# Three phases of an attention kernel merged into one order of slots, with queries and keys projected separately and their scores row-tiled

## The reference, cut to what matters

```
mod = silu(c) @ wmod ; sa, ca, ga, sb, cb, gb = its six parts, one row for each batch
h = layernorm(x) * (1 + ca) + sa
x = x + ga * causal_attention(h)                       # one head of 128: "phase A"
h = layernorm(x) * (1 + cb) + sb
# the light attention, "phase L": windows of 128 rows, 8 heads
q, k, v = rmsnorm(h) @ wq, split(rmsnorm(h) @ wkv)
light = softmax(q k^T / 8) v @ wo                      # in each window and head
# the routing: 2 score vectors of 256 for each batch, 32 in all
for token in (q_token, kv_token):
    s = h @ token
    scores = coor_descent(s)                           # 50 iterations over 32 x 256 numbers
    top_k(scores)                                      # 128 rows as queries; all 256 as keys
# the heavy attention, "phase H": 128 chosen queries against 256 keys, 8 heads
heavy = softmax(q_h k_h^T / 8) (v_h * scores_kv) @ wo_h
x = x + gb * (light + heavy added to the chosen rows)
```

## Time and profile before

| | |
|---|---|
| median of 3 runs | 541.76 us (539.86 to 545.21) |
| profiled execution, its own time | 540.5 us |
| its span, first to last instruction | 538.7 us |
| granted TensorE clock, mean | 0.981 |
| PE busy | 480.9 us (89%), 3805 matmul instructions |
| DVE busy | 387.7 us (72%) |
| ACT busy | 396.4 us (74%) |
| POOL busy | 259.9 us (48%) |

### The profile page before, as it was taken

One profiled execution on the slowest core, in us unless ns is written; L12 is line 12 of the kernel. 1 busy time (PEld: TensorE's weight loads), 2 busy tenths in 40 slices (PEclk: granted clock), 3 DMA queues, 4 the chain that ended last, 5 costly groups with the idle time before them and its releaser, 6 DMA issues.

```text
span 538.7 us, 12047 instructions
## 1 busy us (share of the span) xinstructions
PE 480.9 (89%) x3805; PEld 414.2 (77%) x3805; DVE 387.7 (72%) x1311; ACT 396.4 (74%) x1480; POOL 259.9 (48%) x294
## 2 busy tenths in 40 slices
PE   2498878766999999999999798899999999999995
PEld 1386656545888888888888676798898988888984
DVE  5539999985888888888888798365656656556652
ACT  2269899856999999999999567666666676666662
POOL 6316577772334333334433123454556665556555
PEclk9999999978999999999999889999999999999998
DMA  8740101100000000000000000000000100000101
GB/s 233 258 204 2 31 21 31 31 30 19 2 12 12 12 11 11 12 11 12 11 12 12 12 10 12 21 19 8 12 12 11 16 16 12 12 12 11 16 7 16
DMA packets 18398, 16.42 MB, mean 30 GB/s; under 512 B 1984, under 2 KB 17104, under 8 KB 18080
## 3 DMA queue, kind: packets, MB, share of 16 engines
q1 hardware_dynamic: 14336, 11.83, 6.8%
q0 software_dynamic: 3248, 3.41, 3.7%
q10 hardware_dynamic: 752, 0.40, 0.3%
HBM read 10.36 MB, written 5.28 MB: 29 GB/s over the span
## 4 chain that ended last, share of the span: by engine, by line
PE 69%; DVE 7%; ACT 2%; issue 1%; POOL 1%; POOLq 0%; DVEq 0%
PE bank L651 13%; PE bank L653 10%; PE bank L652 10%; PE bank L884 6%; PE bank L932 6%; PE bank L834 6%; PE bank L916 5%; PE bank L852 5%; PE bank L819 4%; PE bank L949 2%; ACT pr L584 1%; DVE left L1250 1%; DVE top_at L1251 1%; DVE nmx L1218 1%; DVE top_all L1247 1%
## 5 line engine op out<-in xcount | busy, mean ns | idle before, releaser
L402 POOL TENSOR_TENSOR pr<-pr,rinv 128x512 f32<-128x512 f32 x64 | 66.7, 1042 | 134.8 <-DVE rinv L1224 134.7
L417 POOL TENSOR_TENSOR pr<-pr,rinv 128x512 f32<-128x512 f32 x64 | 72.5, 1133 | 76.6 <-DVE rinv L1327 76.4
L584 ACT ACTIVATE pr<-bank,nmx 128x128 f32<-128x128 f32 x256 | 89.7, 364 | 8.0 <-DVE nmx L1218 7.9
L628 ACT ACTIVATE pr<-bank,nmx 128x256 f32<-128x256 f32 x128 | 59.7, 472 | 34.0 <-DVE nmx L1321 33.9
L1218 DVE TENSOR_REDUCE nmx<-bank 128x4 f32<-128x512 f32 x64 | 43.5, 680 | 28.8 <-PE bank L653 27.2
L584 ACT ACTIVATION_READ_ACCUMULATOR pr<-bank,nmx 128x1 f32 x256 | 52.5, 205 | 0.0
L819 PE MATMUL bank<-ident,pr 128*128 128x128 f32 x256 | 39.6, 278 | 5.8 <-POOL pr L402 5.8
L1321 DVE TENSOR_REDUCE nmx<-bank 128x2 f32<-128x512 f32 x64 | 43.8, 684 | 0.7 <-PE bank L653 0.4
L884 PE MATMUL bank<-xq,T_w 128*128 128x128 f32 x256 | 41.8, 286 | 0.4 <-ACT xq L613 0.4
L638 ACT ACTIVATE pt<-bank 128x512 f32<-128x512 f32 x64 | 38.4, 600 | 1.4 <-PE bank L916 1.4
L916 PE MATMUL bank<-ident,pr 128*128 128x128 f32 x256 | 38.5, 273 | 0.4 <-POOL pr L417 0.4
(11 more groups left out here) (231 smaller groups left out, 1506.9 us busy)
## 6 DMA issues: line engine op xcount, KB each, us to landing
mod_bc<-mod_rows_scratch SPq DMA_DIRECT2D x1, 3072.0 KB, 11.1
X<-in_L_attn_x SPq DMA_DIRECT2D x4, 512.0 KB, 10.3
xh_scratch<-xhs SPq DMA_DIRECT2D x16, 128.0 KB, 1.8
out<-X SPq DMA_DIRECT2D x16, 128.0 KB, 1.8
mod_bc<-mod_rows_scratch SPq DMA_DIRECT2D x1, 1024.0 KB, 4.2
wkv_raw<-in_L_ffn_wkv_light SPq DMA_DIRECT2D x1, 512.0 KB, 11.8
wmod_sb<-in_L_wmod ACTq DMA_DIRECT2D x1, 384.0 KB, 5.1
wq_raw<-in_L_ffn_wq_heavy POOLq DMA_DIRECT2D x1, 256.0 KB, 7.5
```

Of the source, the lines that this page charges most:

```text
L402: pool.tensor_tensor(q, q, rinv[k % 4][:, :, None].broadcast_to([P, 4, P]), ALU.mult)\
L417: pool.tensor_tensor(q, q, rinv[k % 4][:, 0:2, None].broadcast_to([P, 2, N]), ALU.mult)\
L584: act.activation(pr[k % 4][:, i * P:(i + 1) * P], ps[2 + k % 2][:, i * P:(i + 1) * P], ACT.Exp, bias=nmx[k % 4][:, i:i + 1], accum_out=sum ...
```

## The change

All three phases stand in one order of 158 slots. `run_slots` walks the slots and calls, for each engine, every stage whose unit is due: A units start at slots 0, 2, 5, 7, 10 ... 37 (`A_AT`), L units one in each slot from slot 14 (`L0`) to 77, H units one in each slot from slot 78 (`H0`) to 141. So from slot 14 to 50 A and L run together. A's stages have new lags (up to 13) and share PSUM banks by `a_bank` and `emptied`.

The product matrices are gone. L projects queries and keys by themselves (`Q_w`, `K_w`, each split once into float32r halves), again with 24 float32r matmuls of 256 columns for a batch, and copies them out of PSUM as plain float32 (`QT`, `KT`; ACT two of four, DVE two of four). There is no `u_hi` and `u_lo`. Its scores are eight float32 matmuls for each window: head 2c lies on partitions 0 to 63 and writes bank 2, head 2c+1 on partitions 64 to 127 and writes bank 3. The two banks are written together for two units, so the next pair of units waits for all exps of the last (`lt["p"]`), and the transposed probabilities use bank 4 alone.

H does the same: `project_q` is four float32 matmuls of 128 columns for a batch, `project_kh` is new with twelve float32r matmuls of 256 columns, and `scores_h` is four float32 matmuls of 256 columns for each pair of units, row-tiled. `pt_evac_h` moves from ACT to DVE.

The iterations of the selection are rewritten: one DVE instruction each (`cd_iteration`, 32 x 256, with a sum), and ACT is needed only three times for exp and ln (`SEGMENTS`). They lie in nine slots (52 to 64, four to six in each), the top rounds in slots 67 to 74, two in each. `xhat` moves from DVE to POOL, and two broadcast loads of gamma fall away.

```
-def steps(phase, units, first, end): ...
-def run_phases(phase_a, phase_l, phase_h, a_to_l, l_to_h): ...
+A_AT = [5 * b // 2 for b in range(B)]
+SCORES_AT = A_AT[-1] + 12
+H0 = SCORES_AT + 29
+L0 = H0 - 4 * B
+END = H0 + 4 * B + 16
+def run_slots(stages):
+    for t in range(END):
+        for phase, lag, f in stages:
+            if phase == "A":
+                if t - lag in A_AT: f(A_AT.index(t - lag))
+            elif phase == "L":
+                if 0 <= t - lag - L0 < 4 * B: f(t - lag - L0)
+            elif phase == "H":
+                if 0 <= t - lag - H0 < 4 * B: f(t - lag - H0)
+            else:
+                f(t)
...
+            def scores(g):
+                if g % 2: return
+                b, w = g // 4, g % 4 // 2
+                window, t = 2 * b + w, slice(w * P, (w + 1) * P)
+                pe.wait_ge(lt["qka"], 2 * b + 2)
+                pe.wait_ge(lt["qkd"], 2 * b + 2)
...
+                at_least(pe, lt["p"], 8 * window)
+                for c in range(4):
+                    for i in range(2):
+                        rows = slice(i * DH, (i + 1) * DH)
+                        mm = pe.matmul(ps[2 + i][:, c * P:(c + 1) * P], QT[b % 2][rows, c, t], KT[b % 2][rows, c, t],
+                                       start=True, stop=True)
...
+            def scores_h(g):
+                if g % 2: return
...
+                at_least(pe, hv["p"], 2 * g)
+                for m in range(2):
+                    for i in range(2):
+                        rows, c = slice(i * DH, (i + 1) * DH), 2 * n + m
+                        mm = pe.matmul(ps[2 + i][:, m * N:(m + 1) * N], QT[b % 2][rows, c, 0:NQ], KT[b % 2][rows, c, :],
+                                       start=True, stop=True)
...
+            def cd_iteration(n):
...
+                dve.scalar_tensor_tensor(cd_min[:, :], cd_e[:, :], u[:, :], inv_k[:, :], ALU.min, ALU.mult,
+                                         accum_out=cd_u[n % 2][:, :]).then_inc(r["u"], 1)
...
+            def pt_evac_h(g):
+                dve.wait_ge(hv["PTp"], g + 1)
...
+                dve.tensor_copy(pt[g % 4][:, :], ps[4][:, :]).then_inc(hv["PT"], 1)
...
+            run_slots([("A", 4, scores_a), ("A", 13, x_transpose), ("L", 7, p_transpose), ("A", 2, h_transpose),
+                       ("L", 0, project), ("A", 3, query_key), ("A", 7, values_a), ("L", 1, project_v),
+                       ("A", 5, p_transpose_a), ("H", 0, row_transpose), ("A", 4, value_a), ("H", 1, project_kh),
+                       ("H", 8, p_transpose_h), ("H", 0, project_q), ("H", 3, project_vh), ("H", 10, values_h),
+                       ("L", 9, values), ("H", 4, scores_h), ("T", 0, heavy_piece), ("H", 12, out_heavy),
+                       ("L", 10, out_light), ("T", 0, selection), ("L", 4, scores)])
```

More of the change, by code:

```diff
@@ L34, in at_least @@
     eng.wait_ge(sem, value)
[L40 to L87, removed]
+A_AT = [5 * b // 2 for b in range(B)]
[7 more added lines that the diff above has]
+            if phase == "A":
+                if t - lag in A_AT:
+                    f(A_AT.index(t - lag))
+            elif phase == "L":
+                if 0 <= t - lag - L0 < 4 * B:
+                    f(t - lag - L0)
+            elif phase == "H":
+                if 0 <= t - lag - H0 < 4 * B:
+                    f(t - lag - H0)
+            else:
+                f(t)
 def adaln_routed_attention(nc, x, w_attn, b_attn, gamma_l, wq_l, wkv_l, wo_l, q_tok, kv_tok,
@@ L137, in adaln_routed_attention @@
         R = 2 * B
+        na_first = sb("na_first", [R, 1])
+        inv_k = sb("inv_k", [R, N])
+        u_first = sb("u_first", [R, 1])
         S_dense = sb("S_dense", [P, C, R])
[L139 to L154, removed]
         selT = sb("selT", [P, 4, R])
@@ L218, in adaln_routed_attention @@
         s4 = [sb(f"s4{i}", [P, 4]) for i in two]
-        early.close()
-        sb = late
-        U = [[sb(f"U{i}{s}", [P, HEADS, N], F32R) for s in ("hi", "lo")] for i in two]
+        QT = [sb(f"QT{i}", [P, 4, N]) for i in two]
+        KT = [sb(f"KT{i}", [P, 4, N]) for i in two]
         V = [sb(f"V{i}", [P, C, HID]) for i in two]
-        pr = [sb(f"pr{i}", [P, 512]) for i in range(4)]
         nmx = [sb(f"nmx{i}", [P, 4]) for i in range(4)]
@@ L269, in adaln_routed_attention @@
         MOD_FIRST = 4
         ROUNDS = NQ // 8
[L271 to L287, removed]
+        HEAVY_PIECES = (4, 6)
@@ new lines, in emptied, with filled @@
+        def emptied(use, b):
+            order = sorted((A_AT[i] + lag, n, u, i) for i in range(B) for n, (u, lag) in enumerate(A_LAGS.items())
+                           if a_bank(u, i) == a_bank(use, b))
+            n = [(u, i) for _, _, u, i in order].index((use, b))
+            return evacuation(*order[n - 1][2:]) if n else (None, 0)
+        def filled(use):
+            last = [b for b in range(B) if A_AT[b] + A_LAGS[use] < L0]
+            return evacuation(use, last[-1]) if last else (None, 0)
@@ L597, in pt_evac_act, with exps_even, exps_odd @@
-            def pt_evac_act(p, k):
-                g = 8 * p + k
-                if not (isinstance(g, int) and g >= ACT_PT):
+                    act.activation(pr[g % 4][:, i * P:(i + 1) * P], ps[2 + g % 2][:, i * P:(i + 1) * P], ACT.Exp,
+                                   bias=nmx[g % 4][:, i:i + 1],
+                                   accum_out=sums[g % 4][:, i:i + 1]).then_inc(lt["p"], 1)
+            def exps_even(g):
+                if g % 2 == 0:
+                    exps(g)
+            def exps_odd(g):
+                if g % 2:
+                    exps(g)
@@ new lines, in project_q @@
+            def project_q(g):
+                if g % 4 != 3:
+                    return
+                b = g // 4
+                pe.wait_ge(hv["xq"], b + 1)
+                if b == 0:
+                    pe.wait_ge(lt["qkd"], 2 * B)
+                    pe.wait_ge(w_scaled, 1)
+                at_least(pe, hv["v"], 2 * b)
+                for c in range(4):
+                    mm = pe.matmul(ps[0][:, c * NQ:(c + 1) * NQ], QH_w[:, c * P:(c + 1) * P], xq[b % 2][:, :],
+                                   start=True, stop=True)
+                mm.then_inc(hv["qp"], 1)
@@ new lines, in iterations, with select_1 @@
+            def iterations(t, part):
+                if t in ITERATIONS_AT:
+                    first, end = ITERATIONS_AT[t]
+                    for n in range(first + 2 * part, min(end, first + 2 * part + 2)):
+                        cd_iteration(n)
+            def select_1(t):
+                iterations(t, 0)
+                if t == SCORES_AT + 2:
+                    cd_start()
+                if TOP_AT <= t < PACK_AT:
+                    top_round(2 * (t - TOP_AT))
+                if t == PACK_AT:
+                    pack_selected()
+                if t == PACK_AT + 1:
+                    keep_selected()
```

1163 lines of the change are left out of this document (574 added, 589 removed).

## The result

The kernel after takes 524.11 us (median of 4 runs, 522.75 to 525.74), the kernel before 542.73 beside it (539.86 to 545.21): a ratio of 0.966, interval 0.960 to 0.972. The forecast was 512, the range 487 to 544. The profiled execution of after took 524.66 us with a span of 522.8.

What follows compares the result with a forecast made beforehand. PE was taken to bound L and H, with time lost in phase A and around the selection; 50 + 166 + 98 + 179 + 17 = 510 us span, so 512 us forecast, range 487 to 544.

Steps and rivals of the forecast that it cites:

- The first rival: Light and heavy scores: the row halves overlap fully, weight loads too, giving 495 us; chance 0.25.
- To slot 14: Start of the kernel: four batches of A and the weight splits put slot 14 at 50 us.
- The price of the light scores: L on PE: sixteen 128-column instructions a window, taken without overlap at 1.9 us; 1.2 with overlap.
- low end: L with overlapping halves: 1.2 us a window, 3.06 a slot, so PE's slots 14 to 50 take 149 us.
- ACT's 131: Slots 14 to 50: ACT's work, 36 L units at 2.08 us plus 11.7 batches of A at 4.79.
- my 166: Slots 14 to 50, A and L: PE bound at 162 us, 2% added for waits, 166 us.
- Slots 50 to 78: L beside the selection: PE needs 95 us, DVE bounds some slots; 3.5 a slot, 98 us.
- The heavy batch: H on PE: a batch falls from 11.54 to 11.2 us, 2.80 a slot, 179 us for 64 slots.
- the second rival: Scores: the halves don't overlap at all, H costs 27 us more, 539 us, no change; chance 0.10.
- the move is free as long as it is covered by PE: H: probabilities' copy moved to DVE, whose 2.3 us a slot lies under PE's 2.80, costs nothing.
- The end: After the heavy slots: 17 us from the last `project_h` to the finish, same as before.
- The third rival: L's two score banks: scores, maxima, exps and next scores form an exposed loop; 545 to 571 us, chance 0.12.

Runs made afterwards that it cites:

- halves in turn: The kernel after with all score matmuls of the lower row half first, then all of the upper, not alternated: 542.65 us, ratio to before 1.003.
- six iterations: The kernel after with 43 of the 49 selection iterations on VectorE left out, output not the reference's: 512.01 us, ratio to before 0.945.
- The bank alone: The kernel after with the light output projection writing bank 5 instead of shared bank 6 from slot 53 on: 518.25 us, ratio to before 0.957.
- the input alone: The kernel after with the selection's exponentials in PSUM, so each iteration has one SBUF input: 516.09 us, ratio to before 0.955.
- both together with the other two: The kernel after with maxima ahead of VectorE's copy, second bank for light output, scatter last and exponentials in PSUM: 503.15 us, ratio to before 0.930.
- no overlap costs 26 us: The kernel after with both heads' heavy scores made from the same 64 rows, output not the reference's: 550.35 us, ratio to before 1.018.
- two different edits: Each against the kernel after: heavy probabilities' copy back on ACT, 517.08 us; heavy maxima ahead of that copy on DVE, 516.65 us.

## Why the prediction was right, and where it was off

Right: faster by more than the measurement's 1%, by 18.6 us where 30 were forecast. The reason given was only a part of it. The forecast kept PE's work about as it was and took the gain from the time in which PE waited in phase A. In the traces PE is busy for 20.1 us less and idle for 4.2 us more than before. A beside L does fill PE (100 to 200 us), but up to the first `row_transpose` PE's idle time falls by only 6.5 us, with 14.9 us of it in slots 50 to 78 beside the selection, and H and the end have 10.7 us more of it than before.

That 512 came so near to 524.1 is in part luck. The kernel that the forecast prices, with no overlap in the light scores and overlap in the heavy ones, is the one with the halves in turn, and it took 542.7. The overlap that the forecast had put aside is worth 18.5 us, and it hides more than half of the 31 us by which the sum was short. The first rival (full overlap) had the light scores right; its 495 us is 29 too low by the terms that the sum missed.

1. **To slot 14**: 50 against 49.2.
2. **The price of the light scores**: I took 1.9 us for a window, the case without overlap; 1.12 was measured, the low end being 1.2. The step that failed is how I used the 64-row instructions of the earlier trace rows. These eight all lie on one half (in the kernel before the line takes one `r0` for a whole piece), so they took 8 x 0.107 + 0.2 in turn and could say nothing on two halves. The rule of the Trainium skill that I put beside a rival ("TensorEngine Tiling (Array Packing)", Key Properties: tiles load and multiply in parallel) agrees with the trace: eight steps of 0.107 for sixteen instructions. Slots 14 to 50 are 151.3 us, close to the 149 of my low end for PE. I had put ACT's 131 so close behind that I gave that rival 155; that was not needed. Without the overlap these slots are 159.5 us (halves in turn) against my 166; sixteen instructions in turn cost 1.64 there and not 1.9.
3. **Slots 50 to 78**: 105.3 against 98. With overlap and the full clock PE has 86 us of work here (28 x 3.06; busy 85.9 with six iterations), so the waits are some 19 us where the sum allowed 3. I called `finish_light` a small one and the iterations work that partly runs ahead; neither what is queued behind them (`tmp`, and through the shared bank 6 the values), nor GpSimd's hold on the second SBUF input, nor the clock that falls in the gaps was in the sum. The bank alone gives 7.6 back, the input alone 8.0, both together with the other two 13.8, each to about 1 us. That the clock might fall in gaps I had named as what would make the forecast wrong, without a price.
4. **The heavy batch**: 11.84 against 11.2. PE's prices were right: eight instructions 1.07 against 1.06, though made of four pairs at 0.215 and not of eight at 0.107 as I wrote; no overlap costs 26 us, against the 27 of the second rival. The step that failed is "the move is free as long as it is covered by PE". I checked VectorE's time in a slot, 2.3 of 2.80, and not its order: the copy waits for PE ahead of maxima whose scores are ready. That is 6 us of the 10, shown by two different edits. The other 0.23 us a batch (11.43 against 11.2) is a mis-sized saving on PE: in the steady part the batch went from 11.53 to 11.38 with the wait gone, 0.15 us instead of the 0.34 in the sum. Which of its prices is too low stays open.
5. **The end**: 39.4 against 28. I took 17 us behind the last `project_h`, a stage that the new order doesn't have; from the last heavy scores (502.4) it is 20.4 us, and the last batch starts at slot 138 with 20 slots to go. Cut at the last `row_transpose`, the kernel before has 27.4 us. The edits took at most 2.8 us off the end; that the rest is the latency of the stages one behind the other is argued and not tested.
6. **The third rival**, the exposed loop over the score banks, is not what costs: PE's wait for ACT before the light scores is 0.4 us in all (4.2 with the bank of its own). But a loop of this kind, scores, maxima, exps, scores, is what the copy lengthened in H, by 1.2 us once in a batch, of which PE had other work for all but 0.4.

## What to carry to other kernels

An engine with a third of its time free can still lengthen a loop: read in which order its pieces stand, and whether the one in front waits for something later than the one behind it has. A row gives a price only for its own pattern, so look in the code at which half, bank or input it used before it is taken against a rule. Where many short instructions fill an engine, ask who is queued behind them and which other engine reads SBUF beside them. And when a forecast comes near, look for the kernel that it really priced: here an experiment was that kernel, and was 31 us off.

## What the hardware showed that I hadn't expected

A VectorE instruction of 0.47 us with two SBUF inputs took 1.13 to 1.30 us when it started during a GpSimd multiplication (1.04 us alone, up to 1.25 then); with one of the inputs in PSUM it was never over 0.474, at no price of its own. Float32 matmuls of 64 rows run in pairs on the two row halves at the price of one instruction on one half, 0.107 us for 128 columns and 0.215 for 256. Runs of eight of 128 columns on one half lose most of that (1.64 us for sixteen instead of 1.12), runs of four of 256 columns don't (1.07 for eight).
